# Moving the last layer's variances of batches 2 to 7 into the FFN of a fused gated-recurrence and ternary-FFN kernel

## The chip, the cores and the metric

The kernel runs on one core of a Trainium2 chip. The metric is the device time of one launch in microseconds; smaller is better. Before the change it is 1538.08 us, the median of 3 runs (1537.69 to 1538.49).

## What is computed

```
h1 = x + fusion(cat(h_fwd, h_bwd))         # x: 8 batches x 512 tokens x 512 features
#   h_fwd, h_bwd: four minGRU layers over layernorm(x), in each direction; per layer
#     z = sigmoid(h Wz + bz); t = tanh(h Wz + bz)
#     scan over tokens: s = clip(1 - z) * s + z * t
#     h = layernorm(s + h) * gamma + beta          (residual from layer 1 on)
out = h1 + ffn(layernorm(h1))
#   ffn: u = gelu(x @ ternary(W_fc).T), 2048 hidden units
#        layernorm over the 2048, * w + b;  @ ternary(W_proj).T
```

What the change touches is the layernorm of the LAST layer of the recurrence. It isn't applied to the states. The fusion product runs on the raw states with weights that already hold gamma and are centred, and each token's row of the product is multiplied by that token's 1/sqrt(variance + eps), once for each direction. So only a variance per token and direction is needed from the states: 128 tokens of one batch (a "unit") need 128 x 2 numbers.

## The kernel before

Two stages follow each other.

*The recurrence.* States lie with features on the 128 partitions (4 groups of 128 features) and 512 tokens along them, in the tiles H. There are 56 jobs (batch, direction, layer), in the order of JOBS (line 48); layer 0 serves both directions in one job. A job is four products of 12 matmuls (mm, line 479), each followed by sigmoid and tanh on ScalarE, a blend and a scan on VectorE (blend, scan) and clip and add on GpSimd. For the layernorm over features the states are turned: tokens (line 505) issues 4 transposes of 128x128 on TensorE for each 128 tokens, into one of five rotating PSUM banks (RING); stats (line 1123) takes bn_stats and bn_aggr of the turned tile on VectorE; inv (line 1606) takes the power -1/2 on GpSimd. In layers 0 to 2 the turned tile is normalised (norm) and turned back (back); in layer 3 nothing but the variance is kept, as rl. The order of all engines is written out by hand as "slots", one job to a slot; tokens of job s stand in slot s+1 after its third and its fourth product. The raw states of layer 3 are also stored to a scratch array in HBM (hs), 1 MB for each batch and direction.

*The FFN.* For each unit u (128 tokens, 32 units) SyncE loads its states hc (128 x 8 x 128: features, 8 groups of both directions, tokens) and input rows xr (load_unit, line 1923), ScalarE rounds hc (whole), VectorE takes the rest (cut), TensorE makes the fusion product in two halves of 12 matmuls, one for each direction (fuse(u, h), line 557). From unit 4 on all halves use one PSUM bank, PS[2]: fuse(u, 1) waits on f_x1 until resid(u, 0) on VectorE (line 1252) has read the first half, and fuse(u+1, 0) until resid(u, 1) has read the second. resid multiplies by rl and adds to the rows; then bn_stats, inv_1 (GpSimd) and unit_norm (VectorE, line 1280) normalise the row, feat turns it, unit_feat and unit_lo split it in two. For each batch b the FFN proper then runs over 16 blocks of 128 hidden units, c = 0 to 15, j = 16 b + c: fc(j) of 8 matmuls, hidden(j) on ScalarE (gelu, scaled and rounded copy gh, square), low_part (gl), total (acc) and squares (acq) on VectorE, and proj(j - 2) of 8 matmuls. While the FFN of batch b runs, the four units of batch b + 1 are fused at c = 2, 5, 8 and 11 (FUSE_AT, line 45): fuse(.,0) and resid(.,0) at that c, fuse(.,1) and resid(.,1) at c + 1. On VectorE the order inside a block is: unit_norm, low_part, total, squares, resid(.,0), resid(.,1), unit_lo, cut, shifted. The sums over tokens for the FFN's own layernorm are taken once a batch (block_sums, moments, deviation).

GpSimd's part of a block: inv_1, addx (adds the bias to the next rows), final (adds the output up) at c = 3 to 6, add_c at c = 10 to 13.

Of the kernel before, what the change touches and what calls it, by code (L numbers as in the profile page):

```python
# [14 lines left out]
NB = 8  # L15
# [29 lines left out]
FUSE_AT = (2, 5, 8, 11)  # L45

# [93 lines left out]

def order(first, pattern):
# [24 lines left out]
for _s in SLOTS:  # L166
# [4 lines left out]
    for _what, _who, _o, _n in RING_SLOT:  # L171
        _i = subject(_who, _s - _o)
        if _i is not None and _what == "T":
            USERS += [("T", _i, _n, 0), ("T", _i, _n, 1)]
# [3 lines left out]
USERS += [("T", LAST, _n, _i) for _n in (0, 1) for _i in (0, 1)]  # L178
# [10 lines left out]
STATS = {u: n + 1 for n, u in enumerate(order(START_STAT, STAT_SLOT) + [("h", LAST, 0), ("h", LAST, 1)])}  # L189
INVS = {u: n + 1 for n, u in enumerate(order(START_INV, INV_SLOT) + [("h", LAST, 0), ("h", LAST, 1)])}  # L190
# [27 lines left out]
def pixart_block(nc, x, wt, cond, fwt, fb, gamma, beta, fct, lnw, lnb, pjt, out):  # L218
# [92 lines left out]
    sb(p2, "pad", [128, 272])  # L311
# [16 lines left out]
    glx = sb(p2, "glx", [128, 4, S], F32R)  # L328
# [62 lines left out]
    s_gb, s_ws = sem("s_gb"), sem("s_ws")  # L391
    f_bt, f_bs, f_sl = sem("f_bt"), sem("f_bs"), sem("f_sl")
# [27 lines left out]
    def _(e):  # L420
# [84 lines left out]
        def tokens(tau, pr):  # L505

            if tau is None:
                return
# [48 lines left out]
        def fuse(u, h):  # L557
# [4 lines left out]
            else:  # L562
# [13 lines left out]
        def feat(u):  # L576
# [10 lines left out]
            r.then_inc(f_t1, 1)  # L587

# [37 lines left out]
        def proj(j):  # L626
# [180 lines left out]
    def _(e):  # L807
# [121 lines left out]

        def unit_feat(u):  # L930
# [12 lines left out]
        def hidden(j):  # L943
# [148 lines left out]
    def _(e):  # L1092
# [8 lines left out]
        def scan(k, m):  # L1101
# [149 lines left out]

        def resid(u, h):
# [796 lines left out]
```

## Time and profile before

| what | value |
|---|---|
| time, median of 3 | 1538.08 us |
| the profiled execution | 1538.64 us, its span 1536.8 us |
| recurrence (to the first fusion product) | about 0 to 868 us |
| FFN of batches 0 to 7 | about 896 us to the end, 82.5 us a batch |
| granted TensorE clock | 1.00 (2.4 GHz) throughout |

Times in the trace are counted from the start of the span; the 1.8 us around the span are in the kernel's time. Consecutive matmuls of the same kind are recorded with overlapping spans, so what one costs is read from the distance between starts and from the chain of work, not from its duration.

### The profile page before, as it was taken

How to read it: one execution, taken by the hardware profiler on the slowest of the kernel's cores; microseconds unless marked ns; L12 is line 12 of the kernel's file. 1: busy time of each engine (PE TensorE's matmuls, PEld its weight loads, DVE VectorE, ACT ScalarE, POOL GpSimd, SP SyncE). 2: the span in 40 equal slices, each digit the busy share in tenths (PEclk: the TensorE clock that was granted, in tenths of full speed). 3: DMA queues.
4: the chain of work that ended last, by engine and by line, in shares of the span. 5: the costliest groups of instructions: out<-in, count | busy, mean ns of one | idle time of the engine just before them, and what ended most of it. 6: DMA issues, size and time to landing. Idle time of an engine off the chain costs nothing.

```text
span 1536.8 us, 22966 instructions
## 1 busy us (share of the span) xinstructions
PE 1515.5 (99%) x7744; PEld 1197.1 (78%) x7744; DVE 1318.8 (86%) x2038; ACT 1021.6 (66%) x1688; POOL 829.7 (54%) x1013
## 2 busy tenths in 40 slices
PE   9999999999999999999999999999999999999998
PEld 6877888888888888888888877777777777777766
DVE  8998999999899988999888887787887877777786
ACT  7988889898687898787987444545454444445364
POOL 5766657678868678676788632241323333332231
PEclk9999999999999999999999999999999999999999
DMA  4211212321302112222143551030202020111000
GB/s 172 76 34 70 93 66 89 120 75 63 123 31 95 41 56 73 79 96 83 35 144 126 197 186 42 1 110 1 90 21 89 21 90 21 62 48 45 25 22 35
DMA packets 73157, 113.20 MB, mean 74 GB/s; under 512 B 5193, under 2 KB 37961, under 8 KB 69970
## 3 DMA queue, kind: packets, MB, share of 16 engines
q1 hardware_dynamic: 72754, 111.21, 21.2%
q8 instruction: 63, 1.03, 0.3%
q10 hardware_dynamic: 288, 0.52, 0.1%
q14 instruction: 52, 0.43, 0.1%
HBM read 73.95 MB, written 37.77 MB: 73 GB/s over the span
## 4 chain that ended last, share of the span: by engine, by line
PE 49%; DVE 3%; ACT 1%; issue 0%; POOL 0%; DVEq 0%; POOLq 0%; ACTq 0%
PE ps L640 15%; PE ps L621 14%; PE ps L572 11%; PE ps L501 6%; PE ps L521 1%; PE ps L586 1%; PE ps L535 1%; DVE bnp L1131 1%; ACT H L875 0%; PE ps L650 0%; DVE yb L1111 0%; DVE H L1119 0%; ACT AH L879 0%; DVE H L1120 0%; DVE ps L1099 0%
## 5 line engine op out<-in xcount | busy, mean ns | idle before, releaser
L501 PE MATMUL ps<-AH,WH 128*128 128x512 f32 x896 | 367.1, 410 | 7.8 <-DVE H L1120 6.1
L501 PE MATMUL ps<-AL,WH 128*128 128x512 f32 x896 | 351.1, 392 | 0.0
L501 PE MATMUL ps<-AH,WL 128*128 128x512 f32 x896 | 349.7, 390 | 0.0
L1604 POOL TENSOR_TENSOR H<-H,yb 128x512 f32<-128x512 f32 x192 | 246.0, 1291 | 8.5 <-DVE yb L1111 1.3
L1111 DVE TENSOR_TENSOR_SCAN yb<-ab,ps 128x512 f32<-128x512 f32 x192 | 232.1, 1209 | 15.5 <-POOL ab L1595 9.1
L949 ACT ACTIVATE g<-ps 128x512 f32<-128x512 f32 x128 | 76.5, 598 | 245.2 <-PE ps L621 245.1
L836 ACT ACTIVATE yb<-ps,ncnd 128x512 f32<-128x512 f32 x224 | 158.1, 706 | 87.9 <-PE ps L501 84.9
L501 PEld LDWEIGHTS ps<-AH,WH 128*128 128x128 f32 x896 | 168.6, 188 | 46.6 <-DVE H L1120 8.6
L1705 POOL TENSOR_TENSOR rs<-mv,nhalf 128x1 f32<-128x1 f32 x32 | 43.0, 1342 | 286.4 <-DVE mv L1278 286.4
L501 PEld LDWEIGHTS ps<-AL,WH 128*128 128x128 f32 x896 | 168.2, 188 | 37.0
L501 PEld LDWEIGHTS ps<-AH,WL 128*128 128x128 f32 x896 | 169.1, 189 | 29.4
L1306 DVE SCALAR_TENSOR_TENSOR gl<-g,wbcol,gh 128x512 fp32r<-128x512 f32 x118 | 116.9, 991 | 86.3 <-ACT gh L959 86.2
L1131 DVE BATCH_NORM_STATS2 bnp<-ps 128x6 f32<-128x512 f32 x256 | 165.3, 687 | 20.4 <-PE ps L521 19.9
L1595 POOL TENSOR_SCALAR ab<-yb 128x512 f32<-128x512 f32 x224 | 139.8, 624 | 71.1 <-ACT yb L836 56.8
L848 ACT ACTIVATE ntok<-ps,nbp,rsp 128x512 f32<-128x512 f32 x192 | 139.9, 788 | 45.5 <-POOL nbp L1620 45.2
L1099 DVE SCALAR_TENSOR_TENSOR ps<-yb,ps 128x512 f32<-128x512 f32 x224 | 152.3, 680 | 18.3 <-ACT ps L837 17.9
L875 ACT ACTIVATE H<-ps,bet,gam 128x512 f32<-128x512 f32 x192 | 155.5, 810 | 5.4 <-PE ps L535 5.2
L1143 DVE TENSOR_TENSOR AL<-ps,AH 128x512 fp32r<-128x512 f32 x224 | 146.1, 673 | 11.8 <-ACT AH L879 11.6
L879 ACT ACTIVATE AH<-ps 128x512 fp32r<-128x512 f32 x224 | 139.8, 629 | 3.2 <-PE ps L535 3.0
L1616 POOL TENSOR_TENSOR rsp<-mvp,nhalf 128x2 f32<-128x2 f32 x96 | 68.2, 710 | 121.3 <-DVE mvp L1134 119.9
L521 PE MATMUL ps<-ident,H 128*128 128x128 f32 x1024 | 131.3, 273 | 1.6 <-DVE AL L1143 0.9
L521 PEld LDWEIGHTS ps<-ident,H 128*128 128x128 f32 x1024 | 117.7, 140 | 16.2 <-DVE AL L1143 1.8
(195 smaller groups left out, 3230.4 us busy)
## 6 DMA issues: line engine op xcount, KB each, us to landing
hs_scratch<-H SPq DMA_DIRECT2D x16, 1024.0 KB, 5.4
hc<-hs_scratch SPq DMA_DIRECT2D x32, 512.0 KB, 4.5
xr<-in_x SPq DMA_DIRECT2D x32, 256.0 KB, 4.6
out<-ob SPq DMA_DIRECT2D x32, 256.0 KB, 2.2
xbuf<-in_x SPq DMA_DIRECT2D x7, 1024.0 KB, 7.8
RAW<-in_wt SPq DMA_DIRECT2D x16, 256.0 KB, 7.3
stg<-in_fct SPq DMA_DIRECT2D x16, 256.0 KB, 3.1
stg<-in_pjt SPq DMA_DIRECT2D x16, 256.0 KB, 2.7
```

The lines of the kernel that those rows point to most:

```text
L501: r = e.matmul(GATE[i % 3][:], w[:, q, m * 128:(m + 1) * 128], a[:, q, :], start=(n == 0), stop=(n == 11))
L521: r = e.transpose(RING[n % 5][:, m * 128:(m + 1) * 128], H[s][:, m, c:c + 128], ident[:])
L572: r = e.matmul(FUSED[u, h][:], a[u % 2][:, q, :], w[:, q, :], start=(n == 0), stop=(n == 11))
L621: r = e.matmul(HIDDEN[j % 2][:], w[q][:, c * 128:(c + 1) * 128], a[b % 2][:, q, :], start=(n == 0), stop=(n == 7))
L640: r = e.matmul(PROJ[t][:], a[BUFFER[j]][:, t * 128:(t + 1) * 128], PJ[c], start=(c == 0 and a is gh), stop=(c == NC - 1 and a is gl))
L836: e.activation(yb[i % 5][:], GATE[c][:], ACT.Sigmoid, bias=ncnd[:, l, m:m + 1], scale=-1.0).then_inc(s_y, 1)
L875: e.activation(H[s][:, m, :], RING[n][:], ACT.Identity, bias=bet[:, m:m + 1], scale=gam[:, m:m + 1]).then_inc(s_h, 1)
L1099: e.scalar_tensor_tensor(GATE[c][:], yb[i % 5][:], 1.0, GATE[c][:], ALU.subtract, ALU.mult, reverse0=True).then_inc(s_p, 1)
L1111: e.tensor_tensor_scan(yb[i % 5][:, rv], ab[c][:, rv], GATE[c][:, rv], 0.0, ALU.mult, ALU.add).then_inc(s_sc, 1)
L1131: e.bn_stats(bnp[:, r, i, 0:6], RING[BANK[u] % 5][:]).then_inc(s_bs, 1)
L1143: e.tensor_tensor(AL[s][:, m, :], RING[BANK[u] % 5][:], AH[s][:, m, :].bitcast(F32), ALU.subtract).then_inc(s_al, 1)
L1604: e.tensor_tensor(H[s][:, m, :], H[s][:, m, :], yb[i % 5][:], ALU.add).then_inc(s_v, 1)
```

## The change

1. tokens, stats and inv are left out for layer 3 of batches 2 to 7 (`turned`, LATE = 8 units): 12 tails (batch and direction), the very last one (LAST) among them, which stood between the two stages.
2. The variances of units 8 to 31 are taken in the FFN, from the states hc that are loaded there anyway. state_squares (ScalarE) squares hc into hsq. state_sums (VectorE) adds up, for each direction and token, the 4 feature groups, of hc and of hsq: two reductions of 128 x 1024. state_blocks turns the sums in blocks of 32 x 32 and reduces them. stat_sums (TensorE) adds the partition blocks with four small matmuls against the selector. factors (VectorE, four tiny operations) makes the variance; state_factors (GpSimd) takes the power; resid(u, 0) waits for it (f_rl).
3. unit_norm moves from VectorE to ScalarE, with a bias nun made on GpSimd.
4. The order at the head of the FFN changes: fuse(4, 0) before feat(3), the constant sums later (j = 4), cut(4) and resid(4, 0) earlier.
5. load_unit is split; states are loaded one unit earlier than rows.

```diff
+def unit_at(b, c, at):
+    u = 4 * b + at.get(c, 4 * NB)
+    return u if LATE <= u < NU else None
+SQUARED_AT = {9: 8, 14: 9, 3: 6, 6: 7}
+SUMMED_AT = {10: 8, 1: 5, 4: 6, 7: 7}
+ADDED_AT = {13: 8, 4: 5, 7: 6, 10: 7}
+LATE = 8
+def turned(t):
+    return t[2] < 3 or 4 * t[0] < LATE
...
         def tokens(tau, pr):
-            if tau is None:
+            if tau is None or not turned(TAILS[tau]):
                 return
...
+            if u + 2 > LATE:
+                e.wait_ge(f_hv, 4 * (min(u + 2, NU) - LATE) - 3)
             for m in range(KC):
                 r = e.transpose(TURNED[:, m * 128:(m + 1) * 128], n1[:, m * 128:(m + 1) * 128], ident[:])
             r.then_inc(f_t1, 1)
+        def stat_sums(u):
+            b, n = (u - 4) // 4, u - LATE
+            e.wait_ge(f_hs, 4 * n + 4)
...
+            for c in range(4):
+                r = e.matmul(TURNED[32 * c:32 * c + 32, 0:4], sel[:], hpart[:, :, c], start=True, stop=True)
+            r.then_inc(f_ht, 1)
...
         feat(2)
-        tokens(LAST, 0)
-        tokens(LAST, 1)
-        sums(0)
+        fuse(4, 0)
         feat(3)
         fc_three_tiles()
-        sums(1)
         for j in range(NB * NC):
             b, c = j // NC, j % NC
             fc(j)
             if b > 0 and c == 1:
                 moments(b - 1)
-            if b + 1 < NB and c in FUSE_AT:
+            if unit_at(b, c, ADDED_AT) is not None:
+                stat_sums(unit_at(b, c, ADDED_AT))
+            if b + 1 < NB and c in FUSE_AT and j > 2:
                 fuse(4 * b + 4 + FUSE_AT.index(c), 0)
+            if j == 4:
+                sums(0)
+                sums(1)
...
+        def state_squares(u):
...
+            e.activation(hsq[:], hc[i][:], ACT.Square).then_inc(f_hq, 1)
+        def unit_norm(u):
...
+            e.activation(n1[:], x1[u % NX1][:], ACT.Identity, bias=nun[:, r:r + 1], scale=rs[:, r, 0:1]).then_inc(f_n1, 1)
...
+        def state_sums(u, of_squares):
...
+            e.reduce_sum(hsum[:, 2 * of_squares:2 * of_squares + 2, :], src[:].rearrange("p (d q) t -> p d t q", d=2),
+                         axis=AX_X).then_inc(f_hs, 1)
+        def state_blocks(u):
...
+            e.transpose(hturn[:].rearrange("p k t -> p (k t)"), hsum[:].rearrange("p k t -> p (k t)")).then_inc(f_hs, 1)
+            e.wait_ge(f_hs, 4 * n + 3)
+            e.reduce_sum(hpart[:], hturn[:].rearrange("p k (b j) -> p k b j", j=32), axis=AX_X).then_inc(f_hs, 1)
+        def factors(u):
...
+            e.tensor_copy(hall[:], TURNED[:, 0:4]).then_inc(f_hv, 1)
...
             if h == 0:
-                if t == 0:
+                if u >= LATE:
+                    e.wait_ge(f_rl, u - LATE + 1)
+                elif t == 0:
                     e.wait_ge(s_rs, max(INVS[("h", TAIL[(b, d, 3)], p)] for d in (0, 1) for p in (0, 1)))
...
         for j in range(NB * NC):
             b, c = j // NC, j % NC
-            if b + 1 < NB and c - 2 in FUSE_AT:
-                unit_norm(4 * b + 4 + FUSE_AT.index(c - 2))
             low_part(j)
+            if unit_at(b, c, ADDED_AT) is not None:
+                factors(unit_at(b, c, ADDED_AT))
             if b > 0 and c == 1:
                 deviation(b - 1)
             if b + 1 < NB and c - 3 == FUSE_AT[3]:
                 unit_lo(4 * b + 7)
             total(j)
             squares(j)
+            if unit_at(b, c, SUMMED_AT) is not None:
+                state_sums(unit_at(b, c, SUMMED_AT), 0)
+                state_sums(unit_at(b, c, SUMMED_AT), 1)
+                state_blocks(unit_at(b, c, SUMMED_AT))
             if c == NC - 1:
                 block_sums(b, 0)
                 block_sums(b, 1)
-            if b + 1 < NB and c in FUSE_AT:
+            if b + 1 < NB and c in FUSE_AT and j > 2:
                 resid(4 * b + 4 + FUSE_AT.index(c), 0)
...
+        def state_factors(u):
...
+            e.tensor_tensor(rl[:, u // 4, :, u % 4], hvar[:, r, :], nhalf[:, 0:2], ALU.pow).then_inc(f_rl, 1)
...
-        def load_unit(u):
+        def load_states(u):
             b, q, i = u // 4, u % 4, u % 2
             if u >= 2:
                 e.wait_ge(f_sp, u - 1)
+            if u >= LATE + 2:
+                e.wait_ge(f_hq, u - 1 - LATE)
+                e.wait_ge(f_hs, 4 * (u - 2 - LATE) + 1)
...
             if u == 2:
                 spread_sums()
-            if u + 5 < NU and u + 5 > 4:
-                load_unit(u + 5)
+            if u + 6 < NU:
+                load_states(u + 6)
+            if u + 5 < NU:
+                load_rows(u + 5)
             if u >= 4:
                 store_out(u - 4)
```

## Rows read from the trace of the kernel before

**Rows 1.** The page, part 1: busy time, share, instructions of TensorE.
```profile
PE 1515.5 (99%) x7744; PEld 1197.1 (78%) x7744; DVE 1318.8 (86%) x2038; ACT 1021.6 (66%) x1688; POOL 829.7 (54%) x1013
```

**Rows 2.** Busy time by stretch: length, then PE, PEld, DVE, ACT, POOL (instructions).
```profile
0.00:866.00 866.00, 850.74 (x4685) 708.75 (x4686) 794.53 (x1308) 715.63 (x1208) 613.58 (x859) 1.00 0.24 85
...
1062.00:1145.00 83.00, 83.00 (x383) 60.55 (x382) 64.45 (x90) 38.12 (x60) 25.94 (x18) 1.00 0.16 52
```

**Rows 3.** Waits of TensorE, 0 to 866 us: total, times, longest.
```profile
PE ps L501 <- DVE H L1120: 6.1, 6, 1.3
```

**Rows 4.** The chain of work at the recurrence's end: start, us, what.
```profile
860.38 3.02 PE ps L501 x12
863.40 0.87 PE ps L521 x8
864.27 2.75 PE ps L501 x12
```

**Rows 5.** Line L521 (tokens), all of it: duration ns min/median/max, first and last start.
```profile
L521 PE MATMUL ps<-ident,H x1024: 270/273/329, 31.8 to 892.5; 128*128 128x128 f32 x171
```

**Rows 6.** Groups by line and shape: busy us, mean ns, idle before.
```profile
L1131 DVE BATCH_NORM_STATS2 bnp<-ps 128x6 f32<-128x512 f32 x256 | 165.3, 687 | 20.4 <-PE ps L521 19.9
...
L1134 DVE BATCH_NORM_AGGREGATE mvp<-bnp 128x2 f32<-128x9 f32 x256 | 40.2, 187 | 0.0
```

**Rows 7.** TensorE in order of time at the head of the FFN, with its idle.
```profile
893.64 0.66 PE L586 MATMUL ps<-ident,n 128*128 128x128 f32 x4 [0.28 <-DVE n L1285]
...
908.07 0.47 PE L572 MATMUL ps<-FUH,hch 128*128 128x512 f32 x1 [0.99 <-DVE x L1269]
```

**Rows 8.** TensorE in order of time, FFN of batch 2: moments, the matmuls beside it.
```profile
1060.34 0.39 PE L640 MATMUL ps<-PJB,gl 128*128 128x512 f32 x1
...
1062.45 0.25 PE L661 MATMUL ps<-part,sel 128*32 128x8 f32 x8
1062.62 0.50 PE L640 MATMUL ps<-PJB,gh 128*128 128x512 f32 x1
```

**Rows 9.** The same: first matmul of fuse(.,1) at c = 3, 6, 9, 12.
```profile
1072.98 0.58 PE L572 MATMUL ps<-FUH,hch 128*128 128x512 f32 x1
...
1089.81 0.59 PE L572 MATMUL ps<-FUH,hch 128*128 128x512 f32 x1
...
1106.59 0.58 PE L572 MATMUL ps<-FUH,hch 128*128 128x512 f32 x1
...
1123.36 0.58 PE L572 MATMUL ps<-FUH,hch 128*128 128x512 f32 x1
```

**Rows 10.** VectorE in order of time, same batch: gl of c = 2, resid(.,0) four times.
```profile
1067.95 0.75 DVE L1306 SCALAR_TENSOR_TENSOR gl<-g,wbcol,gh 128x512 fp32r<-128x512 f32 x1 [1.52 <-ACT gh L959]
...
1069.82 0.75 DVE L1269 SCALAR_TENSOR_TENSOR x<-ps,rl,xr 128x512 f32<-128x512 f32 x1
...
1086.88 0.74 DVE L1269 SCALAR_TENSOR_TENSOR x<-ps,rl,xr 128x512 f32<-128x512 f32 x1
...
1103.44 0.74 DVE L1269 SCALAR_TENSOR_TENSOR x<-ps,rl,xr 128x512 f32<-128x512 f32 x1
...
1120.79 0.74 DVE L1269 SCALAR_TENSOR_TENSOR x<-ps,rl,xr 128x512 f32<-128x512 f32 x1
```

**Rows 11.** VectorE at c = 4 of the same batch, in order of time.
```profile
1080.01 1.52 DVE L1285 TENSOR_SCALAR n<-x,mv,rs 128x512 f32<-128x512 f32 x1
1081.45 1.77 DVE L1306 SCALAR_TENSOR_TENSOR gl<-g,wbcol,gh 128x512 fp32r<-128x512 f32 x1
1083.14 0.68 DVE L1320 TENSOR_TENSOR acc<-acc,g 128x512 f32<-128x512 f32 x1
1083.75 0.68 DVE L1334 TENSOR_TENSOR acq<-acq,sq 128x512 f32<-128x512 f32 x1
```

**Rows 12.** GpSimd beside it: final.
```profile
1081.21 1.46 POOL L1740 TENSOR_TENSOR ob<-ob,x 128x512 f32<-128x512 f32 x1
```

**Rows 13.** Line L1352 (sel), by itself.
```profile
L1352 DVE TENSOR_REDUCE sel<-ident x1: 378/378/378, 885.4 to 885.4; 128x32 f32<-128x128 f32 x1
```

**Rows 14.** VectorE's turn, reduction and a tiny operation, by line and shape.
```profile
L1345 DVE STREAM_TRANSPOSE acct<-acc 128x512 f32<-128x512 f32 x8 | 5.6, 704 | 0.0
...
L1347 DVE TENSOR_REDUCE part<-acct 128x16 f32<-128x512 f32 x8 | 5.5, 687 | 0.3
...
L1394 DVE TENSOR_TENSOR vge<-veg,msq 128x4 f32<-128x4 f32 x8 | 1.3, 164 | 0.8
```

More of the change, by code:

```diff
@@ L172 @@
         _i = subject(_who, _s - _o)
-        if _i is not None and _what == "T":
-            USERS += [("T", _i, _n, 0), ("T", _i, _n, 1)]
+        if _what == "T":
+            USERS += [] if _i is None or not turned(TAILS[_i]) else [("T", _i, _n, 0), ("T", _i, _n, 1)]
         elif _i is not None and (_who == "x" or TAILS[_i][2] < 3):
@@ L327, in pixart_block @@
     xh.append(sb(p2, "xh1", [128, KC, S], F32R))
-    glx = sb(p2, "glx", [128, 4, S], F32R)
+    with ExitStack() as p4:
+        glx = sb(p4, "glx", [128, 4, S], F32R)
+    with ExitStack() as p5:
+        hsq = sb(p5, "hsq", [128, 8, 128])
+        hsum = sb(p5, "hsum", [128, 4, 128])
+        hturn = sb(p5, "hturn", [128, 4, 128])
+    sb(p2, "under", [128, 4, S])
     gh = [sb(p2, f"gh{i}", [128, S], F32R) for i in range(3)]
@@ L391, in pixart_block @@
     s_gb, s_ws = sem("s_gb"), sem("s_ws")
+    f_hq, f_hs, f_ht, f_hv, f_rl, f_un = (sem(n) for n in ("f_hq", "f_hs", "f_ht", "f_hv", "f_rl", "f_un"))
     f_bt, f_bs, f_sl = sem("f_bt"), sem("f_bs"), sem("f_sl")
@@ L561, in fuse @@
                 claim(BANK[("F", u, h)])
-            else:
+            elif u > 4 or h == 1:
                 e.wait_ge(f_x1, 2 * u + h)
@@ L567, in fuse @@
                 e.wait_ge(s_sc, 4 * NJ)
+            if u == 5 and h == 0:
                 e.wait_ge(f_cs, 1)
@@ L587, in feat @@
             r.then_inc(f_t1, 1)
+        def stat_sums(u):
+            b, n = (u - 4) // 4, u - LATE
+            e.wait_ge(f_hs, 4 * n + 4)
+            if u % 4 == 1:
+                e.wait_ge(f_mu, b)
+                e.wait_ge(f_vg, b)
+                e.wait_ge(f_hv, 4 * n - 3)
+            else:
+                e.wait_ge(f_xh, u - 1)
+                e.wait_ge(f_xl, u - 1)
+            for c in range(4):
+                r = e.matmul(TURNED[32 * c:32 * c + 32, 0:4], sel[:], hpart[:, :, c], start=True, stop=True)
+            r.then_inc(f_ht, 1)
         def fc_of_first(t):
@@ L928, in whole @@
             e.activation(hch[i][:], hc[i][:], ACT.Copy).then_inc(f_sh, 1)
+        def state_squares(u):
+            i, n = u % 2, u - LATE
+            e.wait_ge(d_hc[i], 16 * (u // 2) + 16)
+            if n == 0:
+                e.wait_ge(d_hs[3], 64)
+            else:
+                e.wait_ge(f_hs, 4 * n - 2)
+            e.activation(hsq[:], hc[i][:], ACT.Square).then_inc(f_hq, 1)
+        def unit_norm(u):
+            r = u % 2
+            e.wait_ge(f_un, u + 1)
+            if u >= 1:
+                e.wait_ge(f_t1, u)
+            if u == 0:
+                e.wait_ge(s_xs, 4 * NB)
+            e.activation(n1[:], x1[u % NX1][:], ACT.Identity, bias=nun[:, r:r + 1], scale=rs[:, r, 0:1]).then_inc(f_n1, 1)
         def unit_feat(u):
@@ L1071, in _ @@
         whole(2)
+        unit_norm(0)
         whole(3)
         unit_feat(0)
+        unit_norm(1)
         unit_feat(1)
+        whole(4)
+        unit_norm(2)
         unit_feat(2)
+        unit_norm(3)
         unit_feat(3)
-        whole(4)
         for j in range(NB * NC):
@@ L1080, in _ @@
             hidden(j)
+            if b + 1 < NB and c - 2 in FUSE_AT:
+                unit_norm(4 * b + 4 + FUSE_AT.index(c - 2))
+            if unit_at(b, c, SQUARED_AT) is not None:
+                state_squares(unit_at(b, c, SQUARED_AT))
             if b > 0 and c == 2:
@@ L1516, in _ @@
         cut(2)
-        unit_norm(0)
         resid(1, 0)
@@ L1521, in _ @@
         unit_lo(0)
-        unit_norm(1)
         resid(2, 0)
@@ L1527, in _ @@
         unit_lo(1)
-        unit_norm(2)
+        cut(4)
         resid(3, 0)
@@ L1531, in _ @@
         unit_lo(2)
-        unit_norm(3)
-        stats(LAST, 0)
+        resid(4, 0)
         unit_lo(3)
-        stats(LAST, 1)
-        sum_rows()
-        cut(4)
-        sum_part(1)
         for j in range(NB * NC):
             b, c = j // NC, j % NC
-            if b + 1 < NB and c - 2 in FUSE_AT:
-                unit_norm(4 * b + 4 + FUSE_AT.index(c - 2))
             low_part(j)
+            if unit_at(b, c, ADDED_AT) is not None:
+                factors(unit_at(b, c, ADDED_AT))
             if b > 0 and c == 1:
@@ L1820, in _ @@
                 inv_2(b - 1)
-            if j in (4, 7):
-                whole_row((4, 7).index(j))
+            if unit_at(b, c, ADDED_AT) is not None:
+                state_factors(unit_at(b, c, ADDED_AT))
+            if j in (9, 10):
+                whole_row((9, 10).index(j))
             if b + 1 < NB and c - 1 in FUSE_AT:
```

73 lines of the change are left out of this document (59 added, 14 removed).

## The prediction

> **What bounds the kernel now.** I read the page's busy times first, then the busy time by stretch, then who waits for whom, then the engines in order of time in one FFN batch. TensorE is busy 99% of the span [rows 1], and the stretches say where the rest is: 850.7 of 866 us in the recurrence, all of the 83 us of an FFN batch [rows 2]. Of the recurrence's missing 15 us the largest kind of wait that is left after the start is 6.1 us in six pieces behind scans of layer 0 [rows 3]. VectorE has 64.5 of 83 us in an FFN batch [rows 2], so it has idle time there, but the question is where it lies. So every instruction that leaves TensorE is worth its full spacing as long as no one else becomes late, and VectorE's new work is free only while resid stays ahead of TensorE.
>
> How that last thing looks when it fails is in the trace already: at 908.07 us TensorE idles 0.99 us in front of fuse(.,1), waiting for resid(.,0) on VectorE, which works off a backlog at the head of the FFN [rows 7].
>
> **What is removed.** Eight transposes of tokens stand in the chain of work between two products for 0.87 us [rows 4]. All 64 tails have 1024 transposes, 16 each [rows 5]; 12 tails go, 192 transposes, 24 groups of eight. Eleven tails lie in the recurrence: 22 x 0.87 = 19.1 us. VectorE loses for each group 2 x 0.687 + 2 x 0.187 = 1.75 us [rows 6], GpSimd its power: these ran beside, and they go at the same places as the transposes, so VectorE has no new backlog there. The waits behind layer 0 [rows 3] are at other slots; I leave them. Lower end: 15 us if a third of a microsecond of the 0.87 is lost in half of the groups to a scan that is then late; upper end 20.
>
> At the head of the FFN the twelfth tail goes (2 x 0.87 = 1.7 us) and with it VectorE work in a stretch in which VectorE leads: the two waits of 0.28 and 0.99 us should shrink [rows 7]. fuse(4, 0) and the constant sums are only moved. ScalarE takes over four rows to normalise. I take 2.6 us, range 0 to 3. Sum of what is gained: 21.7 us.
>
> **What is added on TensorE.** stat_sums is four small matmuls, as moments is. Moments shows as 0.25 us, and the projection matmul behind it takes 0.50 in place of 0.39 us [rows 8]: 0.36 us together, 24 times (8.6 us; counted by batch below).
>
> **What is added on VectorE.** Per unit: two reductions of 128 x 1024, a turn of 128 x 512, a reduction of 128 x 512, four tiny operations. The turn and the second reduction have rows, 0.70 and 0.69 us [rows 14], the tiny ones 0.16 each with one or two waits [rows 14], 0.5 us in all. The two large reductions have no row. Operations on contiguous elements: 4 elements take 0.164 us, 512 take 0.687 [rows 14]: 1.03 ns an element and 0.16 fixed, so 1024 would take 1.2 us, the lower end. From above: the only reduction that steps (128 bytes from element to element) and sums groups of four, as the new one does, is sel: 128 elements, 0.378 us [rows 13]. (0.378 - 0.16) / 128 = 1.70 ns an element; 1024 x 1.70 + 0.16 = 1.9 us. The new one steps over 512 bytes, q innermost in "p d t q". It is nearest to sel, so I take 1.9 us, and 1.2 as the other end. One state group is then 1.85 + 1.95 + 0.74 + 0.60 = 5.1 us (less a little overlap of neighbours), and 3.7 us at the cheap end.
>
> The Trainium skill, Vector Engine (DVE) Microarchitecture Reference, section Measured stream behaviour on trn2, has a rule on this: a source whose consecutive elements aren't in adjacent pairs costs about 1.73 ns a column in place of 1.05; the sel row agrees [rows 13]. The same section has steps of 24 words at 2.5 ns; by that a state group would be an estimated 6.7 us. It also speaks the other way: a one-source operation that jumped at every element but wrote less than it read ran at the full rate. By that the group would be 3.7 us.
>
> **Where this lands.** The groups stand at the end of blocks c = 1, 4, 7 and 10, right ahead of the blocks in which resid(.,0) must be done before fuse(.,1). How late may resid(.,0) be? It ends at 1070.57, 1087.62, 1104.18 and 1121.53 [rows 10], and fuse(.,1) starts at 1072.98, 1089.81, 1106.59 and 1123.36 [rows 9]: 2.4, 2.2, 2.4 and 1.8 us. Against it:
> - c = 1 into 2: 5.1 us more, 1.5 us of it into the idle time ahead of gl at c = 2 [rows 10]. 3.6 - 2.4 = 1.2 us of wait.
> - c = 4 into 5: no idle time between. 5.1 + 0.5 (factors) + 0.5 (the power on GpSimd gets between the two-operand operations) - 0.3. The 0.3 is all that moving unit_norm gives: it ran 1.52 us from 1080.01, but gh of this block is only there at about 1081.1, and gl starts at 1081.45 [rows 11]. 5.8 - 2.2, less 0.36 by which stat_sums holds TensorE: 3.2 us.
> - c = 7 into 8: the same, less 0.35 us of idle: 5.4 - 2.4 - 0.36 = 2.6; gl may meet final no more: 2.1 us.
> - c = 10 into 11: the same, but gl and acc, both held up by add_c before, are held up once at most (add_c now stands behind state_factors): 4.7 - 1.8 - 0.36 = 2.5, with that 2.0 us.
>
> The delay of one place moves the following blocks as a whole (gl waits for gelu, gelu for fc), so the waits add up: 8.5 us a batch, and 4 x 0.36 for stat_sums: 9.9 us. Gl's 1.77 against 0.75 us is the meeting with GpSimd's final, 1.46 us from 1081.21 [rows 11, 12]; that is why two-operand operations near GpSimd's are uncertain by 1 us each way.
>
> Batches 1 to 5 have all four places, batch 6 three (9.9 - 2.4 = 7.5), batch 0 one (1.8): 5 x 9.9 + 7.5 + 1.8 = 58.8 us. ScalarE has 38 us of work in 83 [rows 2]; four squares and four rows, some 7 us, hide there. SyncE: a load of states one unit ahead now waits for cut two units before, and output stores queue behind it; nobody needs them before the next batch's c = 2. No cost; if that cover were gone, a late store would hold evacuate.
>
> **The sum.** -21.7 + 58.8 = +37 us. The profiled execution is 1538.64, near the median 1538.08: 1538.1 + 37 = 1575 us. With waits of 6 to 11.5 us in place of 8.5: 1560 to 1593.
>
> **Rivals.**
> - *Cheap reads.* The strided reduction runs at the contiguous rate, the group is 3.7 us. Each wait is 1.4 us shorter: 0, 1.8, 0.7, 0.6; with stat_sums 4.5 a batch, 5 x 4.5 + 3.6 + 0.4 = 26.5; minus 21.7: +5, 1543 us (1536 to 1550). For it: 512 elements in 0.687 us. Against it: sel's 0.378.
> - *VectorE absorbs it (the faster side).* The mechanism is slack at the four places: if the group and its neighbours add no more than about 3.3 us each (cheap reads and, since unit_norm is gone, gl and acc no longer held up by GpSimd at c = 4, 7, 10), only the wait at c = 4 is left, 1 us; 5.9 x (1.45 + 1.0) = 14, less 21.7: -7, 1531 us. It decides from 3.3 us on: at 3.7 us the kernel is still slower.
> - *Dear reads.* Stepping costs more than sel shows: 1.5 us more for each group, 23 groups with a place: +35, 1610 us.
> - *The recurrence gives nothing back* (another engine sets the slots): it would be +19 on any of these. Against it: TensorE 98% busy there [rows 2]. It lies in the upper end.
>
> **Chances.** Forecast 0.66; cheap 0.14; absorbed 0.14; dear 0.06. A measurement of this kernel can tell about 0.2% (3 us) from no change. Faster: absorbed 0.14 and 0.02 of cheap. Same: 0.06. Slower: 0.66 + 0.06 + 0.06 = 0.78. Range: the forecast's own, 1560 to 1593, holds some 0.6 of all; to reach 8 in 10 it takes in most of cheap reads: 1539 to 1595.
>
> **What would show it.** The two reductions of 128x1024 at 1.9 us each (1.2: cheap). TensorE idle in front of fuse(.,1), released by VectorE's resid(.,0), at four places a batch, 1.2, 3.2, 2.1, 2.0 us; 46 to 50 us in the wait list; batches of 92 us in place of 82.5; batches 0 and 7 almost unchanged. The first fusion product 19 us earlier. The forecast is wrong if the reductions are under 1.5 us, if VectorE's row in the wait list stays under 20 us, or if the first fusion product isn't earlier by 15 us or more.

## The result and the profile after

The changed kernel takes 1599.2 us (median of 3 runs, 1596.23 to 1600.12) against 1538.08: a ratio of 1.0393, 95% interval 1.0369 to 1.0416, slower. The forecast was 1575 us with a range up to 1595: the direction and the waits came out, but a second cost that hangs on the waits, TensorE's clock, was not in the forecast. The profiled execution took 1600.12 us; its span is 1598.1 against 1536.8 us, 61.3 us more.

The first lines of the page, then the first rows of TensorE's waits (us in total, times, longest) after the change. TensorE's row answers to [rows 1], the second row of the waits to [rows 3]:

```profile
span 1598.1 us, 23333 instructions
...
PE 1526.1 (95%) x7744; PEld 1189.2 (74%) x7744; DVE 1364.2 (85%) x2102; ACT 1065.2 (67%) x1744; POOL 837.4 (52%) x1045
```

```profile
PE ps L604 <- DVE x L1391: 48.5, 24, 3.7
PE ps L532 <- DVE H L1199: 6.1, 6, 1.3
PE ps L566 <- ACT ntok L898: 4.8, 9, 1.5
```

fuse (now L604) waits 24 times for resid(.,0) (now L1391), 48.5 us in all. The waits behind layer 0 are as they were. The third row had 1.8 us, 7 times, in the kernel before (L535 there): two waits of 1.5 us in the recurrence are new. "Moments" below is TensorE's sum over tokens at c = 1 of the next batch; from one moments to the next is one batch.

VectorE in order of time at c = 1 of batch 2 (start, duration, line, what), to set beside [rows 10]:

```profile
1066.62 0.69 DVE L1456 TENSOR_TENSOR acq<-acq,sq 128x512 f32<-128x512 f32 x1
1067.22 2.02 DVE L1343 TENSOR_REDUCE hsum<-hc 128x256 f32<-128x1024 f32 x1
1069.14 2.02 DVE L1343 TENSOR_REDUCE hsum<-hsq 128x256 f32<-128x1024 f32 x1
1071.19 0.71 DVE L1352 STREAM_TRANSPOSE hturn<-hsum 128x512 f32<-128x512 f32 x1
1071.94 0.69 DVE L1354 TENSOR_REDUCE hpart<-hturn 128x16 f32<-128x512 f32 x1
1072.55 0.74 DVE L1428 SCALAR_TENSOR_TENSOR gl<-g,wbcol,gh 128x512 fp32r<-128x512 f32 x1
1073.20 0.68 DVE L1442 TENSOR_TENSOR acc<-acc,g 128x512 f32<-128x512 f32 x1
1073.81 0.68 DVE L1456 TENSOR_TENSOR acq<-acq,sq 128x512 f32<-128x512 f32 x1
1074.41 0.74 DVE L1391 SCALAR_TENSOR_TENSOR x<-ps,rl,xr 128x512 f32<-128x512 f32 x1
```

The group stands in VectorE's queue as one block from 1067.22 to 1072.55 us, 5.3 us, and resid(.,0) comes behind it. Below, what TensorE does after the second wait of this batch (the group at the end of c = 4, the wait in front of fuse(.,1) at c = 6, 33.1 us behind moments), and three stretches of 10 us (PE, PEld, DVE, ACT, POOL busy; then the granted clock, the DMA share and GB/s):

```profile
1096.46 0.77 PE L604 MATMUL ps<-FUH,hch 128*128 128x512 f32 x1 [3.74 <-DVE x L1391]
1097.03 0.63 PE L604 MATMUL ps<-FUL,hch 128*128 128x512 f32 x1
1097.46 0.63 PE L604 MATMUL ps<-FUH,hcl 128*128 128x512 f32 x1
1097.88 0.63 PE L604 MATMUL ps<-FUH,hch 128*128 128x512 f32 x1
...
1099.52 0.40 PE L604 MATMUL ps<-FUL,hch 128*128 128x512 f32 x1
1099.75 0.39 PE L604 MATMUL ps<-FUH,hcl 128*128 128x512 f32 x1
```

```profile
1000.00:1010.00 10.00, 8.94 (x27) 6.79 (x28) 7.41 (x12) 2.52 (x3) 4.41 (x3) 0.66 0.07 26
1090.00:1100.00 10.00, 6.26 (x25) 4.36 (x24) 9.37 (x13) 4.44 (x6) 3.92 (x2) 0.83 0.08 28
1100.00:1110.00 10.00, 10.00 (x52) 7.18 (x51) 7.47 (x13) 4.04 (x7) 5.90 (x6) 1.00 0.33 106
```

Behind the wait of 3.74 us the matmuls of 512 columns start 0.43 us apart, then 0.23 us. The granted clock of that stretch is 0.83 (0.66 at 1000 us, behind the same wait one batch earlier) where every stretch before the change had 1.00 [rows 2]: TensorE ran a part of it at 1.2 GHz in place of 2.4. The records of the clock have eight such parts in the FFN, of 3.4 or 6.8 us, 37.5 us together. Each stands behind a wait: the one at batch 0's end (3.16 us), the six of 3.74 us, and one of 1.97 us. The other waits of 2.02 us and less are not followed by one. Some parts begin just before their wait ends: 2.8 of the 37.5 us lie within waits, where the slower clock costs nothing.

**Where the 61.3 us lie.** The first fusion product starts at 850.89 us against 867.65: -16.8. From there to the moments of the first batch it is +4.7 (117.0 us against 112.3). The six batches that follow take 95.4, 94.3, 96.1, 94.5, 94.3 and 93.7 us, 568.3 against 495.1: +73.3. After the last moments +0.1. In the six batches the waits come to 45.3 us, 23 calls of stat_sums to 9.9 us (0.43 each, below), half of the 28.8 us at the lower clock outside the waits to 14.4: 69.6 of the 73.3. What is left, 3.6 us, has no name.

### The profile page after: what moved, and what is told of

Same layout as the page of the kernel before. It is cut to its first block, busy times and chain, and to the rows that moved or that the text cites. A ratio compares the mean times of both kernels' runs of the same rounds, so it can differ in the third digit from the quotient of the medians.

```text
span 1598.1 us, 23333 instructions
## 1 busy us (share of the span) xinstructions
PE 1526.1 (95%) x7744; PEld 1189.2 (74%) x7744; DVE 1364.2 (85%) x2102; ACT 1065.2 (67%) x1744; POOL 837.4 (52%) x1045
## 3 DMA queue, kind: packets, MB, share of 16 engines
q1 hardware_dynamic: 72754, 111.21, 20.4%
## 4 chain that ended last, share of the span: by engine, by line
PE 37%; DVE 13%; issue 4%; ACT 3%; DVEq 0%; POOL 0%; POOLq 0%; ACTq 0%
PE ps L688 10%; PE ps L670 9%; PE ps L604 9%; PE ps L532 6%; DVE hsum L1343 5%; DVE acq L1456 2%; DVE acc L1442 2%; DVE gl L1428 1%; DVE x L1391 1%; ACT gh L1030 1%; DVE hturn L1352 1%; PE ps L566 1%; ACT g L1019 1%; PE ps L552 1%; PE ps L620 0%
## 5 line engine op out<-in xcount | busy, mean ns | idle before, releaser
L1428 DVE SCALAR_TENSOR_TENSOR gl<-g,wbcol,gh 128x512 fp32r<-128x512 f32 x118 | 107.1, 908 | 84.8 <-ACT gh L1030 84.8
L898 ACT ACTIVATE ntok<-ps,nbp,rsp 128x512 f32<-128x512 f32 x192 | 140.1, 790 | 45.4 <-POOL nbp L1741 45.3
L604 PE MATMUL ps<-FUH,hch 128*128 128x512 f32 x256 | 114.3, 447 | 48.5 <-DVE x L1391 48.5
L1210 DVE BATCH_NORM_STATS2 bnp<-ps 128x6 f32<-128x512 f32 x208 | 134.4, 687 | 16.0 <-PE ps L552 15.8
L887 ACT ACTIVATE ps<-ps,cnd 128x512 f32<-128x512 f32 x192 | 130.9, 682 | 0.0
```

Of the source, the lines that this page charges most:

```text
L604: r = e.matmul(FUSED[u, h][:], a[u % 2][:, q, :], w[:, q, :], start=(n == 0), stop=(n == 11))
L898: e.activation(ntok[w % 2][:, 2 * pr + i, :], RING[BANK[("T", tau, pr, i)] % 5][:], ACT.Identity, bias=nbp[:, r, i:i + 1], scale=rsp[:, r, ...
```

## The experiments

Theory at the start: the waits come from the length of VectorE's group and from its place ahead of resid(.,0), and the clock falls because TensorE waits. Rivals: the reading isn't to blame (the place is), VectorE has no room at all, the clock falls because of the small matmuls. All times are medians beside a kernel before of 1537.84 to 1537.99 us.

**1. Contiguous reductions.** The sums are over four neighbouring tokens in place of the four feature groups, so what comes out isn't the variances; as many elements are read and written.

```
-            e.reduce_sum(hsum[:, 2 * of_squares:2 * of_squares + 2, :], src[:].rearrange("p (d q) t -> p d t q", d=2),
-                         axis=AX_X).then_inc(f_hs, 1)
+            e.reduce_sum(hsum[:, 2 * of_squares:2 * of_squares + 2, :].rearrange("p d (k t) -> p (d k) t", k=4),
+                         src[:].rearrange("p k (t q) -> p k t q", q=4), axis=AX_X).then_inc(f_hs, 1)
```

> The changed kernel, except that the two large reductions of state_sums read four neighbouring tokens of one feature group in place of one token of four feature groups (steps of 4 bytes in place of 512; the same 1024 elements in, 256 out). The variances are then wrong and the output with them; all else is as it was. Theory (the stepping read makes the reduction dear, TensorE waits at four places a batch, and the granted clock falls behind the longest of the waits): the reductions take 1.2 us in place of 2.0, the waits in front of fuse(.,1) fall from about 8 to 3 us a batch (0, 1.9, 0.5, 0), no wait is over 3 us, the granted clock stays at 1.00, and the time is 1542 to 1552 us. Rival (the reduction is dear for another reason, such as its 256 outputs or what GpSimd does beside it): 2.0 us a reduction and 1595 to 1600 us. Rival (the clock falls for any idle of TensorE): the waits shrink but the granted clock still shows stretches at half, 1555 us or more.

1559.23 us, ratio 1.0137 (1.0120 to 1.0154). The reductions by line (busy, mean ns; the changed kernel's pair first, then this one's), and TensorE behind its longest wait:

```profile
L1343 DVE TENSOR_REDUCE hsum<-hc 128x256 f32<-128x1024 f32 x24 | 48.7, 2030 | 0.0
L1343 DVE TENSOR_REDUCE hsum<-hsq 128x256 f32<-128x1024 f32 x24 | 47.7, 1988 | 0.0
```

```profile
L1343 DVE TENSOR_REDUCE hsum<-hc 128x256 f32<-128x1024 f32 x24 | 29.0, 1210 | 0.0
L1343 DVE TENSOR_REDUCE hsum<-hsq 128x256 f32<-128x1024 f32 x24 | 29.0, 1208 | 0.0
```

```profile
1082.85 0.76 PE L604 MATMUL ps<-FUH,hch 128*128 128x512 f32 x1 [2.27 <-DVE x L1391]
1083.41 0.63 PE L604 MATMUL ps<-FUL,hch 128*128 128x512 f32 x1
```

1.6 us less per group takes the waits of a batch from 7.9 to 2.7 us (2.27 and 0.39), and the batch from 94.3 to 88.8. The time is 7 us over my range and fits the rival that expected half clock behind any idle of TensorE (1555 us or more): in all six batches 3.4 us at half speed follow the 2.27 us of waiting. (Not behind any idle, though: the waits of 0.4 and 1.58 us have none behind them.) The cost of stepping, with what hangs on it, is 40 of the 61 us.

**2. TensorE kept busy.** The changed kernel with some 30 extra matmuls a batch into a free accumulator, ahead of the waits, which change no result.

```
+FILL = {(1, 3): 4, (1, 6): 15, (1, 9): 7, (1, 12): 4, (0, 12): 13}
...
+            for i in range(n):
+                e.matmul(HIDDEN[(j + 1) % 2][:], FC[i % 4][:, 0:128], xh[(j // NC) % 2][:, i % 4, :], start=True, stop=True)
```

> The changed kernel with matmuls of no use put where TensorE waits: behind fc(j) at c = 3, 6, 9 and 12 of batches 1 to 6, 4, 15, 7 and 4 of them, and 13 at c = 12 of batch 0, into the PSUM bank that fc(j + 1) overwrites. The waits are as long as before, TensorE only works in them. Theory (some 19 us of the 61 are the granted clock, at half for 37.5 us behind waits of over 3 us): the granted clock is 1.00, batches take about 92 us in place of 94.5, the time is 1576 to 1585 us. Rival (the clock is only a sign of the waiting and costs nothing of its own, the rest being in stat_sums or in waits that the list doesn't show): 1597 to 1605 us, since work is only added. Rival (half clock comes from elsewhere): the same stretches at half stay.

1586.87 us, ratio 1.0319 (1.0303 to 1.0334). The clock of the core (span, mean granted clock):

```profile
core 0: 1584.2 us, clock 1.000
```

VectorE is as late as before; TensorE works off useless matmuls while it waits, the clock never falls, and 12.3 us come back, which leaves the time 2 us above the expected range. So the clock is a cost of its own, at least 12.3 us of it; the batches are 93.0 us, where 82.5 + 7.9 of waits + 1.7 of stat_sums make 92.1, so the extra matmuls seem to cost some 0.9 us a batch themselves, 5 in all. With these the clock's share is some 17. Of the 37.5 us at half clock 34.7 lie outside the waits, and half of that is 17.4. The Trainium skill, TensorE: Matmul & The Clock Gate, section Terms, reckons the penalty as time at the reduced clock times the share of pulses withheld; that would be 18.8 us, and this pair of runs agrees with it to 2 us.

**3. The last batch alone.** LATE is 28 in place of 8: only batch 7's variances by the new way.

```
-LATE = 8
+LATE = 28
```

> The changed kernel with LATE = 28: only batch 7's variances are taken in the FFN, those of batches 2 to 6 in the recurrence as before the change; ScalarE's rows and the new order at the head stay. Theory (each tail gives 1.6 us in the recurrence, each place in the FFN costs 2 to 5 us): the head gives 2 to 4 us, the tail (7,0,3) 1.7, batch 5's c = 10 costs 1.5, batch 6 some 11; time 1541 to 1547 us, batches 1 to 4 at 82.5 us. Rival (the FFN is slower because of the rows on ScalarE, the longer queue on SyncE or the new order): batches 1 to 4 over 84 us, and 1555 us or more.

1552.38 us, ratio 1.0092 (1.0077 to 1.0107). Batches 1 to 4 are back at 82.5 us; the next is 87.9 (a wait of 3.23 us), the one after 95.3 (1.07, 3.74 and 1.93 us), and the clock is at half for 13.6 us in three parts. The waits and 1.7 us of stat_sums make 11.7 us, half of the 12.3 us at the lower clock outside the waits 6.1: together 17.8 of the 18.2 that these two batches are over 165. The cost sits with the units, then, and not with the number of batches; batch 6's three places alone are 12.8 us. The expectation was too low by 5 us: by the clock, and by the first place (the 3.23 us), where I had counted on 1.5.

**4. The sums behind resid(.,0).** They move from c = 1, 4, 7, 10 to c = 2, 5, 8, 11, behind resid(.,0) of that block.

```
-SUMMED_AT = {10: 8, 1: 5, 4: 6, 7: 7}
+SUMMED_AT = {11: 8, 2: 5, 5: 6, 8: 7}
```

> The changed kernel with VectorE's state sums put behind resid(.,0) of c = 2, 5, 8 and 11 in place of the ends of blocks 1, 4, 7 and 10. The same instructions, stepping reads included. Theory (what costs is where the 5.4 us lie, ahead of resid(.,0), and not their sum): resid(.,0) is in time, waits in front of fuse(.,1) under 1 us a batch, VectorE busy some 79 of 84 us, granted clock 1.00, batches 84 to 85 us, and the time is 1525 to 1534 us, less than before the change. Rival (VectorE as a whole has no room for 21 us more a batch): batches of 88 us or more, waits in front of other matmuls (proj, feat, fuse(.,0)), 1550 us or more.

1565.35 us, ratio 1.0179 (1.0164 to 1.0194): 34 us faster than the changed kernel, but 31 us above my expectation and in the range of the rival (no room, 1550 us or more). The waits, and the busy time of one batch (columns as above; 86.80 is VectorE):

```profile
PE ps L604 <- DVE x L1391: 12.6, 13, 1.3
PE ps L620 <- ACT n L998: 10.0, 7, 1.5
PE ps L604 <- DVE hcl L1329: 7.8, 6, 1.3
```

```profile
1055.00:1145.00 90.00, 85.31 (x410) 60.57 (x410) 86.80 (x118) 45.41 (x69) 30.11 (x26) 1.00 0.15 47
```

In place of 49.8 us of waits in 25 pieces (the 48.5 and one of 1.3 at the head) there are 30.4 us in 26, none above 1.5 us, and the clock stays at 1.000: all of its loss is gone. But VectorE is busy 86.8 of 90 us; it is now the bound of the batch. Its work, 64.5 us of 83 before [rows 2], no longer leaves it room. A part of that is new: the tiny hmean (L1364) now runs beside GpSimd's work and takes 1209 ns on average, hvar (L1370) 649 ns, where both took 161 in the changed kernel.

**5. Shorter sums, behind resid(.,0).** Experiment 4 with each strided reduction as two additions of rows, which read neighbours.

```
-            e.reduce_sum(hsum[:, 2 * of_squares:2 * of_squares + 2, :], src[:].rearrange("p (d q) t -> p d t q", d=2),
-                         axis=AX_X).then_inc(f_hs, 1)
+            halves = src[:].rearrange("p (d k q) t -> p d k q t", d=2, k=2)
+            pair = hturn[:].rearrange("p (d q) t -> p d q t", d=2)
+            e.tensor_tensor(pair, halves[:, :, 0], halves[:, :, 1], ALU.add).then_inc(s_th, 1)
+            e.wait_ge(s_th, 2 * n + of_squares + 3)
+            e.tensor_tensor(hsum[:, 2 * of_squares:2 * of_squares + 2, :], pair[:, :, 0], pair[:, :, 1],
+                            ALU.add).then_inc(f_hs, 1)
```

> The state sums stand behind resid(.,0), as in the kernel with the moved sums (1565.35 us, batches of 89.8 us, VectorE busy 86.8 of 90), and each strided reduction of 1.99 to 2.03 us is two two-source additions of whole rows of 128 (of 512 and of 256 results; acc's 512 take 0.68 to 0.8 us), so about 1.05 us. What is computed is the same, in another order of the sum. Theory, that VectorE had no room left: its work in a batch falls by 4 x 1.9 = 7.6 us to some 79, the 4.7 us of waits in a batch shrink to at most 1, batches of 85 to 86 us, 1538 to 1546 us in all, clock 1.00. Rival, that those waits come from the small operations of factors (1.2 us each beside GpSimd) and from ScalarE's n: the waits stay at 4 to 5 us a batch, 1560 to 1566.

1531.73 us (5 runs, 1530.93 to 1532.11), ratio 0.996, interval 0.9947 to 0.9974: faster than both kernels, by 6 us than the one before and by 67 than the changed one, and 6 us below the range I had expected, since the waits went altogether. The rows of the additions (ns, least, median, most), and the waits of TensorE over the whole run:

```profile
L1349 DVE TENSOR_TENSOR hsum<-hturn x48: 424/425/427, 941.3 to 1430.8; 128x256 f32<-128x256 f32 x48
L1347 DVE TENSOR_TENSOR hturn<-hc x24: 671/675/684, 940.6 to 1428.8; 128x512 f32<-128x512 f32 x24
```

```profile
PE ps L532 <- DVE H L1199: 6.1, 6, 1.3
PE ps L566 <- ACT ntok L898: 4.7, 9, 1.5
...
PE ps L604 <- DVE x L1397: 0.6, 1, 0.6
```

1.1 us in place of 2.0, and no wait is left in the six batches; they take 84.2 us each. That shows room as the reason for experiment 4's waits, and not the tiny operations by themselves: hmean still takes 1208 ns here. Against 82.5 there are 1.7 us a batch without any wait, which is 0.43 us for each of the four stat_sums (experiment 8). This kernel's balance: -17.1 us at the first moments, +9.9 over six batches (505.0 us against 495.1), -7.2 in the span.

**6. The same additions, at the places of the change** (experiment 5 with SUMMED_AT as in the changed kernel).

> The additions of the kernel with moved sums and additions (1531.73 us, no wait in front of fuse(.,1)), but at the places of the change, ahead of resid(.,0). VectorE's group is then some 3.6 us a unit, against 3.9 with the contiguous reductions at the same places (1559.23 us, one wait of 2.27 us a batch, each followed by 3.4 us at half clock). Theory, that place and reading each give a part: one wait of 1.9 to 2.2 us a batch; 1553 to 1558 us if the clock falls behind it again, 1543 to 1547 if it stays. Rival, that only the price of the group matters and not its place: no waits, 1531 to 1534 us.

1571.43 us, ratio 1.0212 (1.0195 to 1.0229). Neither reading foresaw it: 40 us above experiment 5, and 12 above the contiguous reductions, whose group is about as long. TensorE waits 28.8 us in all in place of 17.6 there, with the same 20.5 us at half clock, so it is the waits that are longer. The row of the first addition, and VectorE and GpSimd in order of time at batch 0's c = 10:

```profile
L1347 DVE TENSOR_TENSOR hturn<-hc x24: 680/684/1774, 936.1 to 1462.6; 128x512 f32<-128x512 f32 x24
```

```profile
936.15 1.77 DVE L1347 TENSOR_TENSOR hturn<-hc 128x512 f32<-128x512 f32 x1
937.96 1.40 DVE L1349 TENSOR_TENSOR hsum<-hturn 128x256 f32<-128x256 f32 x1
939.46 0.69 DVE L1347 TENSOR_TENSOR hturn<-hsq 128x512 f32<-128x512 f32 x1
```

```profile
935.85 3.23 POOL L1866 TENSOR_TENSOR x<-x,cB 128x512 f32<-128x512 f32 x2 [0.17 <-POOL cB L1858]
```

While GpSimd's two-operand operations run, the additions take 1.77 and 1.40 us; as soon as they are over, 0.69. The same happens at c = 10 of five later batches (1.41 and 1.60 us), and the wait in front of the next fuse(.,1), which experiment 1 has only in batch 0, is 1.45 us there. The changed kernel's reductions at 935.19 and 937.15 took 2.04 and 2.01 us beside the same GpSimd work, as anywhere else: with one operand they aren't held up. The Trainium skill, SBUF — State Buffer, section SBUF: two separate sides, has the rule for two inputs: VectorE's operation with two SBUF inputs and a GpSimd one that reads SBUF shut each other out, and whichever starts first keeps the other waiting for its whole length. These rows agree: VectorE's additions take 0.9 to 1.1 us longer, less than the 1.3 us of one GpSimd addition at c = 10. Place counts twice, then: for what comes behind, and for what runs beside. The waits of 2.35 us are followed by half clock in four batches of six, batch 0's of 4.31 us too.

**7. stat_sums twice, on experiment 4, and 8. on experiment 5.** Its four matmuls are issued a second time; the result is the same.

```
-            for c in range(4):
+            for c in list(range(4)) * 2:
```

> The kernel with the moved sums with the four small matmuls of stat_sums issued twice (the same result is written again), 24 times. It prices them. The prediction's 0.36 us a unit gives 1565.35 + 8.6 = 1574 us. The other reading, that each costs some 0.6 us since the loads of the selector don't overlap, gives 1580. If TensorE has idle time there in any case, it stays at 1565.

> The kernel with moved sums and additions with the four small matmuls of stat_sums issued twice, 24 times. There TensorE waits for nobody in the batches, so this prices them, which the same step on the kernel with moved sums couldn't (its waits took the extra time in). From its batches (84.2 us against 82.5 in the kernel before, four units each) stat_sums costs 0.43 us: 1531.73 + 10.3 = 1542 us. The prediction's 0.36 gives 1540.4. Rival, that the 1.7 us a batch come from something else, for example the longer wait of fuse for its operands, and the small matmuls are nearly free: 1532 to 1535.

On experiment 4: 1564.66 us (1565.35 without). That tells nothing, since VectorE bounds there. On experiment 5, where it doesn't: 1532.93 us (1532.51 to 1533.57) against 1531.73, so 1.2 us for 24 x 4 matmuls, 0.05 us for each call. Its line, with what the weight load sat idle for:

```profile
L635 PEld LDWEIGHTS ps<-hpart,sel x384: 106/111/113, 947.3 to 1436.5; 128*32 128x32 f32 x192
...
  issue: 10.2, 24
```

The idle time is 10.2 us, 24 times, with eight matmuls a call and with four alike (the row of experiment 5 has the same two numbers). stat_sums costs 0.43 us for being there, and hardly anything for its matmuls. Both numbers of the expectation (1542 and 1540.4 us) fell, since they took the price for that of the matmuls; the time is the rival's (1532 to 1535), whose reason holds in half: the matmuls are nearly free, yet the 1.7 us a batch are theirs, as a pause ahead of them. TensorE in order of time in experiment 5, with stat_sums and at a block without it:

```profile
1098.07 0.60 PE L670 MATMUL ps<-xl,FCB 128*128 128x512 f16 x2
1098.59 0.24 PE L635 MATMUL ps<-hpart,sel 128*32 128x4 f32 x8
1098.77 0.50 PE L688 MATMUL ps<-PJB,gh 128*128 128x512 f32 x1
...
1102.07 0.60 PE L670 MATMUL ps<-xl,FCB 128*128 128x512 f16 x2
1102.32 0.58 PE L604 MATMUL ps<-FUH,hch 128*128 128x512 f32 x1
```

Counted from the start of fc's last row, the next product starts after 0.25 us without it; with it the small ones start after 0.52 us and the product after 0.70. What makes the pause isn't settled.

**9. Without the reads.** The 46 strided reductions behind the first unit's are left out; a copy of two columns stands for each, so the variances are not the states'. All else stays.

```
+            if n > 0:
+                e.tensor_copy(hsum[:, 2 * of_squares:2 * of_squares + 2, 0:1], src[:, 0:2, 0:1]).then_inc(f_hs, 1)
+                return
```

> The changed kernel with the 46 strided reductions after the first unit's left out (a copy of two columns stands for each, so the variances are wrong); transposition, block sums, stat_sums, factors, the order and all else stay. Theory, that the reads alone bring the waits and with them the clock: no wait above 1.5 us in front of fuse(.,1), granted clock 1.00, and 1538 - 17 - 2 + 24 x p for stat_sums: 1528 with p = 0.36 us, 1534 with p = 0.6. Rival, that a part of the waits comes from what else stands on VectorE and ScalarE (transposition and block sums 1.4 us, factors 0.6, n on ScalarE): 1545 to 1555 with waits of 1 to 2 us.

1537.7 us, ratio 1.000 (0.9991 to 1.0009), between the theory (1528 to 1534) and the rival (1545 to 1555). Its waits for resid:

```profile
PE ps L604 <- DVE x L1394: 5.2, 7, 4.0
```

4.0 of the 5.2 us are one wait, at 944 us, behind the first unit, which kept its two reductions; 6.8 us at half clock follow. In the six batches each wait is 0.2 us and the period 84.45. By the first moments this one unit has cost 5.9 us against experiment 5 (968.7 against 962.8 us), and the two times differ by 6.0 us in all. So at these places the reads alone make the waits: turn, block sums and factors leave 0.2 us. One unit's group is enough to lose a third of what the recurrence gives.

**10. The group alone.** The kernel before, with the two reductions (both of the states), turn and block sums at the places of the change. The result isn't used; no stat_sums, no factors, TensorE's turns kept.

```
+            for i in (0, 1):
+                e.reduce_sum(hsum[:, 2 * i:2 * i + 2, :], hc[u % 2][:].rearrange("p (d q) t -> p d t q", d=2),
+                             axis=AX_X).then_inc(s_th, 1)
```

> The kernel before with the state group alone put in at the places of the change (c = 1, 4, 7, 10; both reductions read the states, since there are no squares; transposition and block sums follow; nothing uses the result). It has no stat_sums, no factors, keeps TensorE's turns in the recurrence, and VectorE still makes n. Theory: waits as in the changed kernel or longer, since VectorE also has 1.5 us of n per unit, 51 to 70 us in all, and the granted clock at half speed behind the longer ones, 19 to 30 us: 1605 to 1635. Rival, that the clock falls because of something else in the change (the small matmuls of stat_sums, the other order): waits of 51 to 60 us with the clock at 1.00, 1588 to 1598.

1638.17 us, ratio 1.0653 (1.0638 to 1.0667), 3 us over the upper end:

```profile
PE ps L586 <- DVE x L1300: 75.3, 25, 7.2
```

12.3 us of waits a batch in place of 7.9. The wait of c = 4 is 6.6 to 7.2 us, and its cause is not all the group: the states, whose load this kernel leaves where it was, come late there, and VectorE itself waits 3.79 us for them:

```profile
1108.71 3.80 DVE L1276 TENSOR_REDUCE hsum<-hc 128x256 f32<-128x1024 f32 x2 [3.79 <-DMA hc<-hs_scratch]
```

So the size says little on the group's own price. The last wait of a batch, 2.71 us for 1.10, has no such load in front; there VectorE makes n as well. The clock is at half for 68 us, 22 of them within the waits. There is no stat_sums and no new order here, so the fall of the clock needs neither. With experiment 2, where the same waits are filled and the clock stays up, this leaves TensorE's idle time as what makes it fall.

## Why the prediction was wrong

The forecast had the right waits at the right places and charged each at its own length. It had no term for the matmuls at half clock behind them, 17.4 us, and that is what put the time outside the range.

- **The strided read was right.** Forecast 1.9 us by sel [rows 13], measured 2.03 and 1.99; contiguous 1.21 (forecast 1.2). (2.01 - 0.16) / 1024 is 1.81 ns an element. The 1.73 ns of the Trainium skill, Vector Engine (DVE) Microarchitecture Reference, section Measured stream behaviour on trn2, holds here to 5%. Its one-source operation with jumps at the full rate, which would have made the group 3.7 us, is not borne out by this reduction, and neither are its 2.5 ns.
- **The waits were right.** Forecast 1.2, 3.2, 2.1, 2.0 us a batch, measured 1.08, 3.74, 1.97 and 1.10; in the list 48.5 us where 46 to 50 were forecast. The last was 0.9 too high, the second 0.5 too low. Batch 0's one wait is 3.16 us and not 1.4: acc and acq ahead of the group take 1.76 and 1.79 us beside GpSimd's whole_row, which the change moves to this very place (from j = 4 and 7 to 9 and 10) and which the prediction doesn't mention. That the list's total came out so well is in part luck: batch 0 was 1.8 us too low and the six batches 3.6 too high.
- **The step that failed: a wait was priced at its own length.** The trace of before had granted clock 1.00 in every stretch shown, and no wait in the FFN above 1.0 us, so nothing in the sum stood for a fall. Each wait of 3 us and more is followed by 3.4 or 6.8 us at half clock, which cost up to 1.7 or 3.4 us again. That is some 17 of the 24 us that were missing. There was no rival with this mechanism, though the long wait was forecast at its place and size; with 17 us on it the sum is 1592.
- **stat_sums was low, and for another reason.** 0.43 us against 0.36, 24 times: 1.7 us. The forecast read 0.25 us of matmuls and 0.11 of a longer successor [rows 8]; experiment 8 shows that the matmuls are the cheap part and the pause the dear one, so the rows' durations were the wrong thing to read. The starts would have shown it. In the kernel before, moments stands at 1062.45 and the next product at 1062.62 [rows 8], 0.70 us behind fc's last row; a block later that distance is 0.24:

```profile
1061.92 0.60 PE L621 MATMUL ps<-xl,FCB 128*128 128x512 f16 x2
...
1065.93 0.59 PE L621 MATMUL ps<-xl,FCB 128*128 128x512 f16 x2
1066.17 0.58 PE L572 MATMUL ps<-FUH,hch 128*128 128x512 f32 x1
```

- **The recurrence gave less.** 16.8 of 19.1 us (range 15 to 20). Two tails' rows by ScalarE, at 462.35 and 669.03 us, are now waited for 1.47 and 1.45 us, and two at 0.33:

```profile
462.35 0.44 PE L566 MATMUL ps<-ident,ntok 128*128 128x128 f32 x2 [1.47 <-ACT ntok L898]
```

  Without these 3.6 us it is 20.4, or 0.93 for a group of eight; the chain's 0.87 [rows 4] may leave out the change from one kind of product to another and back. I had left such lateness to the lower end of the range. What made these rows late is not looked into.
- **The head gave less.** 1.8 of 2.6 us: the +4.7 there are a wait of 3.16, 3.0 for the clock and 0.43 for stat_sums, less 1.8. The twelfth tail's 1.7 are in these; of the two waits that should have shrunk [rows 7] the one of 0.99 us is gone, but the one of 0.28 has grown to 1.27, now for n on ScalarE:

```profile
878.23 0.66 PE L620 MATMUL ps<-ident,n 128*128 128x128 f32 x4 [1.27 <-ACT n L998]
```

- **The sum.** -21.7 + 58.8 were forecast, +37.1. Measured +61.3, 24.2 more: 2.3 less from the recurrence, 0.8 less from the head, 1.7 more for stat_sums, 1.8 more for batch 0's wait, 17.4 for the clock and 3.6 without a name, but 3.6 less for the waits of the six batches (45.3 against 5 x 8.5 + 6.4). That makes 24.0.
- **The rivals.** "Cheap reads" at 1543 us is experiment 1, at 1559: its waits came (2.27 and 0.39 for 1.8 and 0.7), and the clock, which this rival left out too, takes most of the rest (half of 20.5 us, less what lies in the waits). "Absorbed" at 1531 us needed a group of about 3.3 us at the places of the change. Experiment 6 has about 3.6 us there (more where GpSimd holds it up) and takes 1571; experiment 5 has the same group behind resid(.,0) and takes 1531.73. That its time is the rival's number is chance: the rival left the group where it was, and counted on no gain from another place.

## What to carry to other kernels

Where the trace of before has no long wait, price a wait of TensorE of 2 us and more twice: by its length, and by the slower matmuls behind it. Short waits have only the first price: experiment 4 still waits 30.4 us, in pieces of at most 1.5 us, and loses nothing to the clock. When work is put in front of a producer on an engine that has idle time in sum, first try the other side of the producer, and make the work shorter by reading neighbours: here the one alone left 27 us, the other alone 21 or 33, and both together turned 61 us of loss into 6 of gain.

## What the runs showed of the hardware beyond the forecast

- When the granted clock falls to 1.2 GHz in the FFN, over all runs here. Waits of TensorE of 6.5 to 7.2 us: in 6 of 6, for 6.8 or 10.2 us. Waits of 3.1 to 4.3 us: in 12 of 12, for 3.4 or 6.8 us. 2.71 us: in 4 of 5. 2.33 to 2.35 us: in 4 of 6. 2.27 us: in 6 of 6. 1.93 to 2.02 us: in 2 of 4. 1.80 us and less: in none. Each of the 34 falls before the last matmul begins within such a wait or less than 2 us behind it.
- Putting four small matmuls between two large products costs 0.43 us, four more of them 0.05.
- VectorE's additions of two operands take 1.4 to 1.8 us in place of 0.42 to 0.69 beside GpSimd's two-operand work, tiny ones 1.2 in place of 0.16; its reductions of one operand are unchanged there.
